# The down product's last block of 64 rows kept twice and multiplied as two column halves in two row groups

## What is computed

```python
x = x + xattn(layernorm(x), ctx_1024, ctx_1024, w_q, w_k, w_v, w_o)
x = x + attn(layernorm(x), Wq, Wk, Wv, Wo, bo)

def fp4_linear(x, w):                        # w_down: 256 x 704
    return einsum('bsk,nk->bsn', fp4_quant_dequant(x), fp4_quant_dequant(w))

n = layernorm(x)
h = silu(fp4_linear(n, w_gate)) * fp4_linear(n, w_up)      # 704 wide
x = x + fp4_linear(h, w_down)                              # back to 256
```

## Time and profile before

| | us |
|---|---|
| median of 3 runs | 543.1 (543.04 to 544.62) |
| the profiled execution, its own time | 545.09 |
| the profiled execution, span from first to last instruction | 543.2 |

### The profile page before, as it was taken

The page is one execution under the profiler, slowest core; times in us unless marked ns, Lnnn a source line. Parts: engine busy times, 40 slices in busy tenths (PEclk is TensorE's granted clock), DMA queues, the critical chain, the costliest instruction groups (busy, mean ns, idle before and its releaser), DMA issues.

```text
span 543.2 us, 19544 instructions
## 1 busy us (share of the span) xinstructions
PE 527.3 (97%) x8270; PEld 429.4 (79%) x8270; DVE 444.9 (82%) x860; ACT 208.3 (38%) x415; POOL 48.3 (9%) x86
## 2 busy tenths in 40 slices
PE   8999989999999999999998899999999999999996
PEld 7777968898788988889877767777777777787775
DVE  5666978898988899888973589898888888889883
ACT  2232313232332323323343654554544445544232
POOL 6101000000000000000200111111111111101120
PEclk9999989999999999999999999999999999999999
DMA  7983330333102221022220000000000000000001
GB/s 267 385 207 89 97 89 1 96 96 90 49 28 78 78 78 39 39 78 78 78 78 4 2 1 3 10 10 10 10 10 10 10 10 10 10 10 10 13 0 34
DMA packets 25774, 31.09 MB, mean 57 GB/s; under 512 B 14608, under 2 KB 22672, under 8 KB 23696
## 3 DMA queue, kind: packets, MB, share of 16 engines
q1 hardware_dynamic: 25744, 30.68, 17.5%
HBM read 28.57 MB, written 2.10 MB: 56 GB/s over the span
## 4 chain that ended last, share of the span: by engine, by line
PE 88%; DVE 4%; issue 3%; ACT 3%; DMA 1%; SPq 0%; POOL 0%; DVEq 0%; POOLq 0%; ACTq 0%
PE bank L1376 13%; PE bank L488 11%; PE bank L466 11%; PE bank L457 11%; PE bank L513 10%; PE bank L1351 8%; PE bank L1413 5%; PE bank L504 4%; PE bank L1401 3%; ACT x_oT L628 2%; PE bank L1436 2%; PE bank L1422 2%; PE bank L1329 2%; PE bank L1310 1%; PE bank L1370 1%
## 5 line engine op out<-in xcount | busy, mean ns | idle before, releaser
L488 PE MATMUL bank<-xwv,x_xcT 128*128 128x512 f32 x128 | 60.6, 616 | 1.7 <-issue 0.8
L466 PEld LDWEIGHTS bank<-x_xcT,xwk 128*128 128x128 f32 x512 | 59.5, 192 | 2.8 <-DMA xwk<-in_L_xattn_w_k_dram 1.1
L466 PE MATMUL bank<-x_xcT,xwk 128*128 128x128 f32 x512 | 59.9, 275 | 1.7 <-DMA xwk<-in_L_xattn_w_k_dram 0.9
L457 PE MATMUL bank<-x_xcT,xwq 128*128 128x128 f32 x512 | 59.8, 275 | 0.0
L457 PEld LDWEIGHTS bank<-x_xcT,xwq 128*128 128x128 f32 x512 | 58.5, 192 | 0.0
L513 PE MATMUL bank<-xwo,x_oT 128*128 128x256 f32 x256 | 58.0, 380 | 0.0
L513 PEld LDWEIGHTS bank<-xwo,x_oT 128*128 128x128 f32 x256 | 47.4, 190 | 5.8
L644 ACT COPY x_k_blocks<-bank 64x512 f32<-64x512 f32 x32 | 18.6, 580 | 86.0 <-PE bank L466 85.8
L1351 PE MATMUL bank<-wdT,f_hqT 128*128 128x256 f32 x192 | 45.6, 386 | 0.2 <-ACT f_hqT L1654 0.2
L488 PEld LDWEIGHTS bank<-xwv,x_xcT 128*128 128x128 f32 x128 | 24.0, 193 | 27.6 <-issue 24.0
L1376 PE MATMUL bank<-wuT,f_xqT 128*128 128x192 f32 (+1 forms) x128 | 40.6, 460 | 0.0
(11 more groups left out here) (165 smaller groups left out, 952.3 us busy)
## 6 DMA issues: line engine op xcount, KB each, us to landing
x_ctx_slab<-in_ctx_dram SPq DMA_DIRECT2D x16, 1028.0 KB, 4.8
out_dram<-f_out SPq DMA_DIRECT2D x15, 128.0 KB, 1.7
xall<-in_x_dram SPq DMA_DIRECT2D x1, 1280.0 KB, 14.4
x_first_keys<-in_ctx_dram SPq DMA_DIRECT2D x16, 80.0 KB, 5.2
xwk<-in_L_xattn_w_k_dram SPq DMA_DIRECT2D x1, 1024.0 KB, 5.0
xwq<-in_L_xattn_w_q_dram SPq DMA_DIRECT2D x1, 1024.0 KB, 7.1
xwv<-in_L_xattn_w_v_dram SPq DMA_DIRECT2D x1, 1024.0 KB, 9.2
xwo<-in_L_xattn_w_o_dram SPq DMA_DIRECT2D x1, 1024.0 KB, 13.0
```

The lines of the kernel that those rows point to most:

```text
L457: last = nc.tensor.matmul(bank67[:, j // 4, (j % 4) * P:(j % 4 + 1) * P], xwq[:, k, j * P:(j + 1) * P], xcT[:, k, :], start=(k == 0), stop ...
L466: last = nc.tensor.matmul(bank[2 + j // 4][:, (j % 4) * P:(j % 4 + 1) * P], xwk[:, k, j * P:(j + 1) * P], xcT[:, KD + k, :], start=(k == 0 ...
L488: last = nc.tensor.matmul(bank45[:, half, :], xcT[:, KD + k, :], xwv[:, k, half * 512:(half + 1) * 512], start=(k == 0), stop=(k == KD - 1))
```

## The change

The last chunk of 64 rows is held twice in `f_hqT` and in `wdT`: in rows 0 to 63 and again in rows 64 to 127, in place of the zeros. In the loop every chunk is multiplied as two calls of 128 columns, the first into bank 4, the second into bank 5. Chunks 0 to 4 use all 128 rows in both calls. For the last chunk the first call takes rows 0 to 63 (`tile_position` (0, 0)) and columns 0 to 127, the second rows 64 to 127 (`tile_position` (64, 0)) and columns 128 to 255. `add_out` reads the two banks. `multiply_down`, which the last four tiles use, keeps 256 columns a call, and its last chunk takes 64 rows. ACT gets one more copy for each tile and one more of the weights; two memsets of GpSimd go.

```diff
-                        nc.gpsimd.memset(wdT[:, FC - 1, :], 0.0).then_inc(s_clear, 1)
                         nc.gpsimd.memset(a_v[:], 1.0).then_inc(s_clear, 1)
-                        nc.gpsimd.memset(f_hqT[:], 0.0).then_inc(s_clear, 1)
...
-                            nc.scalar.copy(dst, wt_bank[n % len(wt_bank)][0:rows, 0:width]).then_inc(s_wtc, 1)
+                            turned_rows = wt_bank[n % len(wt_bank)][0:rows, 0:width]
+                            if rows == FR:
+                                nc.scalar.copy(wdT[FR:P, FC - 1, :], turned_rows)
+                            nc.scalar.copy(dst, turned_rows).then_inc(s_wtc, 1)
...
-                    act.wait_ge(s_clear, 3)
+                    act.wait_ge(s_clear, 1)
...
-            down_bank, late_down_bank = bank45[:, 1, 2 * P:2 * P + D], bank[3][:, 0:D]
+            down_banks, late_down_bank = bank45[:, :, 2 * P:2 * P + D // 2], bank[3][:, 0:D]
...
-                    multiply_down(down_bank).then_inc(s_f_d, 1)
+                    multiply_down_in_halves().then_inc(s_f_d, 1)
 
                 def multiply_down(into, c0=0, c1=FC, opens=True):
                     for c in range(c0, c1):
-                        last = nc.tensor.matmul(into, f_hqT[:, c, :], wdT[:, c, :],
+                        rows = slice(0, P if c < FC - 1 else FR)
+                        last = nc.tensor.matmul(into, f_hqT[rows, c, :], wdT[rows, c, :],
                                                 start=(opens and c == 0), stop=(c == FC - 1))
+                    return last
+
+                def multiply_down_in_halves():
+                    for c in range(FC):
+                        for i in range(2):
+                            rows = slice(0, P) if c < FC - 1 else slice(i * FR, (i + 1) * FR)
+                            cols = slice(i * D // 2, (i + 1) * D // 2)
+                            last = nc.tensor.matmul(down_banks[:, i, :], f_hqT[rows, c, :], wdT[rows, c, cols],
+                                                    start=(c == 0), stop=(c == FC - 1),
+                                                    tile_position=(rows.start, 0))
                     return last
...
+                    short = h_bank[1][0:FR, (FC - 5) * P:(FC - 4) * P]
                     nc.scalar.copy(f_hqT[:, 4:FC - 1, :], turned(h_bank[1], FC - 5))
-                    return nc.scalar.copy(f_hqT[0:FR, FC - 1, :], h_bank[1][0:FR, (FC - 5) * P:(FC - 4) * P])
+                    nc.scalar.copy(f_hqT[FR:P, FC - 1, :], short)
+                    return nc.scalar.copy(f_hqT[0:FR, FC - 1, :], short)
...
-                    nc.vector.tensor_tensor(f_out[:], down_bank, tile_of(t), ALU.add).then_inc(s_f_out, 1)
+                    nc.vector.tensor_tensor(f_out[:].rearrange("p (i n) -> p i n", i=2), down_banks,
+                                            tile_of(t).rearrange("p (i n) -> p i n", i=2), ALU.add).then_inc(s_f_out, 1)
```

More of the change, by code:

```diff
@@ L189, in perceiver_layer @@
                                    wdT[0:rows, cs[0]:cs[-1] + 1, :].rearrange("p c d -> p (c d)")))
+        assert 2 * FR == P
         ahead = {}
```

## The result

| | before | after |
|---|---|---|
| median of the runs | 543.22 us (542.65 to 544.62, 6 runs) | 553.42 us (552.22 to 556.68, 6 runs) |
| the profiled execution, its own time | 545.09 | 553.61 |
| its span | 543.2 | 551.9 |

The kernel is slower: ratio 1.019, 95% interval 1.0174 to 1.0207. That is 10.2 us more, where 4.2 were forecast; 553.4 lies outside the range of 545.3 to 549.3. The sign and the loop were right.

A forecast was written before the change was run, and what follows sets the result against it. PE was taken to bound the kernel, filling all 14.51 us of a loop pass. 2.8 (passes) + 1.2 (late products) + 0.16 (ACT copy) = 4.2 us on 543.1 gave 547.3 us, range 545.3 to 549.3.

The forecast's parts named there:

- Steps 1 to 3: Loop pass: full chunks' halving +0.07, short chunk's overlap -0.21, two 64-row tile switches +0.39; +0.25 us, 14.51 to 14.76.
- staggered halves: Short chunk in the loop: strict program order makes two rounds three, +1.3 us, 548.6 us; chance 0.14.
- no overlap: Short chunk in the loop: four rounds, or loads one after the other as well, 2.7 more, 550.0 us; chance 0.05.
- loads hidden: Tile switches: each costs only its 0.09 us hole, 1.2 us in all, 544.3 us; chance 0.08.
- the other side: Loop's tile switches: full-width 64-row pair counts as no other mode, switches cost nothing, 541.6 us; chance 0.05.
- Step 4: Twelve loop passes: eleven at +0.25 and the last at +0.06, 2.8 us.
- step 5: Four late down products in the drain, unpaired, pay only tile switches: 0.26, 0.34, 0.39 and 0.19, together 1.2 us.
- Step 6: ACT's extra copy per tile: hidden in the loop, +0.16 us once in the drain, nothing for the last tile.
- Step 7: The rest: DVE's addition from two banks and GpSimd's two memsets at the start, nothing.

The follow-up runs named there:

- b_halves: Kernel before, code moved back 24 instructions, all six down-product chunks in column halves in two banks, last one keeping 128 rows: 543.1 us, one run.
- a_one_group: Changed kernel, code moved back 24 instructions, both halves of the short chunk taken from rows 0 to 63: 550.65 us, ratio 1.015.
- a_short_first: Changed kernel, code moved back 24 instructions, short chunk multiplied first instead of last in the loop: 546.4 us, one run.
- a_skip_232: Changed kernel with a branch at PE's start jumping over a never-run block of 232 instructions: 549.45 us, ratio 1.0105.
- b_skip_256: Kernel before with a branch at PE's start jumping over a never-run block of 256 instructions: 544.92 us, ratio 1.0021.
- b_copy_up: Kernel before with one more ACT copy of the 64 short rows, into the upper 64 partitions of an unread tile: 543.93 us, one run.
- b_skip_280: Kernel before with a branch at PE's start jumping over a never-run block of 280 instructions: 554.37 us, ratio 1.0178.
- a_code_back: Changed kernel, nine identity products at the start replaced by one and two of four times the width, 24 PE instructions fewer: 550.28 us, ratio 1.011.
- a_skip_256: Changed kernel with a branch at PE's start jumping over a never-run block of 256 instructions: 552.77 us, ratio 1.0173.
- b_code_on: Kernel before with 48 already-met waits (24 instructions in the trace) added ahead of the first loop: 553.77 us, ratio 1.0196.

## Why the prediction was wrong, step by step

**Steps 1 to 3, a pass: right, 14.76 forecast, 14.77 measured.** The parts were right too, not only their sum. Halving the full chunks is + 0.09 for all six (`b_halves`), + 0.07 for five by the same rate. The short passes start in pairs; the way into them is 205 ns between starts, to the second round 206, out again 202, and the load behind is no longer covered: L1435 begins with 1.13 us as L1422 did behind small tiles. `a_one_group` gives the overlap as 0.22, `a_short_first` one switch as 0.195. The rivals "staggered halves", "no overlap", "loads hidden" and "the other side" all fall with these numbers. The Trainium skill's page "TensorE: Matmul & The Clock Gate", section "The mechanism", calls matmuls strictly first in, first out; this trace doesn't agree where row groups differ, since two products start 7 ns apart and the other two 206 ns later, which I read as the first passes of both calls and then the second ones.

**Step 4, twelve passes: 2.8 forecast, 2.9 measured.** From the values of the loop's first pass (334.15 us in before, 331.79 in after) to those of the drain the kernel after falls back by 2.9 us. Right within what was claimed.

**Steps 5 and 6, by the drains of `a_skip_232` against `b_skip_256`.** Both chains at the full clock, in time differences of the same points:

| | forecast | measured |
|---|---|---|
| first late product | 0.26 | 0.11 |
| second | 0.34 | 0.34 |
| ACT's copies ahead of the third | 0.16 | 0.38 |
| third | 0.39 | 0.39 |
| last | 0.19 | 0.20 |
| last tile's copy | 0 | 0.30 |
| sum | 1.34 | 1.72 |

The switches were sized right. What step 5 had wrong is how much the hole behind the first late product covers: besides its 0.10 to 0.13 us also the 0.19 by which the transposes behind it get shorter. Step 6 took 0.16 us from the distance of two copies that both go into the lower partitions; the new one goes into the upper, and that costs 0.38. It also said that the last tile's copy "has time beside the passes of L1351". It has not: ACT starts the three copies at 540.58, 540.86 and 541.13 us in `a_skip_232`, and PE, which is at its last calls, waits for them. Their rows in the chain of `a_skip_232`, where before has one of 1.74 us for all eight passes:

```profile
540.54 0.86 PE bank L1362 x4
541.41 0.03 issue
541.44 1.34 PE bank L1362 x4
```

0.86 + 0.03 + 1.34 is 2.23, less 1.74 and the switch's 0.20: 0.30 us. `b_copy_up`, which has the copy and no 64-row tile, shows the same 0.3 there. With 2.9 for the passes the change itself is 4.6 us. The forecast of 4.2 was short by 0.4 us here, and the range would have held that. That the medians of the two shifted kernels give 4.5 is partly luck: the missing stop near 290 us takes 1.1 away, and the slower executions of `a_skip_232` add to it.

**Step 7, "the rest: nothing": this is the step that failed.** Its list ended with DVE and GpSimd. The twelve further products of the loop's body were priced by their run time, and their place in the code was put at nothing without being named. Against before's trace: the 128 values take 1.22 + 2.55 + 0.23 = 4.00 us instead of 1.25, 2.75 more, with PE standing still where the next instruction load is late. The low clock behind it takes 1.35 on the eight products of L1389 (3.91 against 2.56) and 0.33 on L246 (1.00 against 0.67). That is 4.4 us, more than the whole forecast. `b_skip_280` and `a_skip_232` show that the place of the code brings and removes it.

**And the clock at the longer hole.** The copies leave PE 1.92 us between two starts instead of 1.54, and in the profiled execution of after the clock was granted at 0.50 behind that: the third late product takes 3.93 instead of 2.59 us, and L1370 1.22 instead of 0.70, 1.9 us in all, of which 0.2 are the switch. The six traces that have a hole of 1.54 there (among them before, `b_halves` and `b_skip_256`) show no drop behind it; of seven with 1.92 (after, `a_code_back`, `a_one_group`, `a_short_first`, `b_copy_up`, `a_skip_256`, `a_skip_232`) two do. So it is not a fixed price. That the longer hole brings it is not shown: two of seven against none of six can be chance, and stretches of low clock stand elsewhere in these traces too. What decides between the executions stays open, and the spread of `a_skip_232` (its profiled execution 547.17 without a drop, the other three 549.4 to 549.8) fits it but doesn't show it, since those three have no trace. Their clock over the whole span is on record, 0.996 to 0.997 against 1.0 in the profiled one, but not where it fell.

Together for the profiled executions, from the same point of the loop to the end: 2.9 for the passes, 2.75 and 1.7 for the hole and its clock, 0.06 for the first late product, 0.35 for the second, 0.38 for the copies, 2.06 for the third and what follows it, 0.8 for the last tile. That is 11.0 us, and the 8.7 of the spans with the 2.4 by which after was ahead give the same within the rounding. In the last tile 0.3 of the 0.8 is neither switch nor copy (a row "issue" of 0.15, and L1331 with 0.38 instead of 0.22); `a_skip_232` hasn't got it, and its cause stays open. The medians differ by 10.2: less than this one pair of traces, as they would if not every execution has the drop at the third product.

**How the hole comes about** is an inference from the traces. In after the packet that loads the next instructions starts at 505.99 us, 1.05 us behind the start of the values, and PE takes its first new instruction at 508.71, 2.7 later. In before the packet starts at 505.50, but the end of the loaded code lies 24 places later, among the products of L1376. These take 0.32 us each (2.56 / 8), so PE has work for some 2.5 us there, and no gap shows. The 128 small products of the values are 256 instructions and go by in 1.25 us. When a load's 256 instructions are nearly all such products, the next one has no time to come; when they are spread over two loads, it has. That each load is 256 instructions was not measured: a shift by 257 places leaves things nearly as they were where one by 24 does not, and other sizes of a block were not tried. Nor does the count close to the last place. The two kernels with the branch lie one place further on, which should leave no fewer products behind the hole; they have two left, after and `b_code_on` three. The Trainium skill's page "Runtime: NRT & Kernel Launch", section "Instruction fetch mechanics", gives blocks of 256 instructions and calls the cost of crossing one mostly hidden. The packets of 16 KB go with that size. Mostly hidden holds for most of the twenty such packets of a trace, but not for all: one crossing costs 2.4 to 2.6 us here, a second 0.4 to 1.9.

No kernel was found that beats before. The place of its code is already a good one for the drain: of the shifts tried none was faster. Near 290 us it is not: a kernel before with its code there 24 places earlier and the drain where it is was not run, and by the traces it should save about 1.1 us (an estimate, 13.89 us from those values to the next ones in `a_skip_232` against 14.99 in `b_skip_256`).

## What to carry to other kernels

A change in a loop's body moves all code behind it. Where some 250 short instructions run in little over a microsecond, as here, look for an "issue" row in the chain that stands within one line, and compare two versions only after shifting one by an unused block; otherwise a change is given credit or blame for its place. Of a change to tile shapes, count the switches first: each costs 0.2 us here, nearly two passes of 128 columns, and one can be had for nothing by putting the odd tile next to work that has left the full tile already. And take the price of a copy from a row that reads and writes the same partitions as the new one will.

## What the runs showed of the hardware that was not expected

- A stop of PE of 2.44 to 2.55 us (1.94 in `b_code_on`) inside a run of independent 32 x 32 products, by the place of the code alone. Behind it the granted clock was at its lower level in all four traces that have the stop, for 3.4 us in three and 6.8 us in `b_code_on`. A second stop, near 290 us, is 0.41 to 0.96 us, 1.66 to 1.91 with the code 24 places later, and gone with it 24 places earlier.
- ACT's copy of 64 partitions of PSUM into the upper 64 of SBUF does not overlap with the copies before and behind it: 0.27 us from start to start instead of 0.16.
- Two calls of 64 rows and 128 columns in different row groups start their float32 passes 7 ns apart, and both second passes 206 ns later: 0.50 us for the four with entry, against 0.72 in one group. Entering and leaving such tiles cost 0.195 us each, so the pair is worth it only if it saves more than what its switches take.
